# A decoder kernel: narrow attentions with queries and keys projected dimension-major and placed by way of DRAM

## The reference, cut to what matters

```
q = rope(x @ Wq)    k = rope(src @ Wk)    v = src @ Wv        # src: x, or the context
probs = softmax(q k^T / 4)                                    # causal in the self-attention
x = layernorm(x + (probs v) @ Wo)                             # cross-attention adds a bias
```

## Time and profile before

| | us |
|---|---|
| median of three runs (3670.48 to 3684.72) | 3678.97 |
| time of the profiled execution | 3678.92 |
| its span, first to last instruction | 3677.3 |
| PE busy / DVE / ACT / POOL | 3309.4 / 2046.3 / 1330.3 / 569.4 |

### The profile page before, as it was taken

One profiled execution on the slowest core, in us unless ns is written; L12 is line 12 of the kernel. 1 busy time (PEld: TensorE's weight loads), 2 busy tenths in 40 slices (PEclk: granted clock), 3 DMA queues, 4 the chain that ended last, 5 costly groups with the idle time before them and its releaser, 6 DMA issues. The chain is left out here.

```text
span 3677.3 us, 54612 instructions
## 1 busy us (share of the span) xinstructions
PE 3309.4 (90%) x19817; PEld 2550.5 (69%) x19818; DVE 2046.3 (56%) x4960; ACT 1330.3 (36%) x2944; POOL 569.4 (15%) x621
## 2 busy tenths in 40 slices
PE   7999999999999999987957899889898867999995
PEld 6889888888888788873425565545555435787784
DVE  3555655566666666632155666666667545343445
ACT  0444434443444344421113343435445443122110
POOL 1333322222222222024140111210000000000000
PEclk7999989999999999968988999989999978999998
DMA  5211110111111010024440000000000011000001
GB/s 190 53 53 53 53 53 30 35 35 30 30 35 35 28 31 30 1 104 160 137 119 32 2 3 2 28 2 22 5 5 5 2 46 24 24 12 11 23 11 46
DMA packets 110616, 146.80 MB, mean 40 GB/s; under 512 B 23712, under 2 KB 72864, under 8 KB 109288
## 3 DMA queue, kind: packets, MB, share of 16 engines
q1 hardware_dynamic: 95904, 110.80, 9.5%
q0 software_dynamic: 14480, 32.91, 2.9%
HBM read 100.55 MB, written 42.08 MB: 39 GB/s over the span
## 5 line engine op out<-in xcount | busy, mean ns | idle before, releaser
L554 ACT ACTIVATE probs_w<-probs_w,low_w 128x256 f32<-128x256 f32 (+1 forms) x512 | 242.9, 475 | 590.3 <-DVE low_w L599 590.3
L1861 DVE TENSOR_REDUCE mx_n<-bank 128x6 f32<-128x768 f32 (+1 forms) x256 | 279.8, 1093 | 148.8 <-PE bank L1638 78.5
L1769 ACT ACTIVATE probsT_n<-bank 128x768 f32<-128x768 f32 (+1 forms) x256 | 235.8, 921 | 273.1 <-PE bank L1650 272.7
L572 DVE TENSOR_TENSOR probsT_lo_w<-bank,probsT_hi_w 128x384 fp32r<-128x384 f32 (+1 forms) x256 | 159.7, 624 | 124.7 <-ACT probsT_hi_w L537 124.0
L518 PE MATMUL bank<-wo_hi_w,oT_hi_w 128*128 128x512 f32 x512 | 211.9, 414 | 2.1 <-issue 2.1
L1632 PE MATMUL bank<-kT_n,qT_n 48*128 48x256 f32 (+1 forms) x1024 | 123.5, 321 | 94.3 <-DVE mx_n L1861 91.5
L518 PE MATMUL bank<-wo_hi_w,oT_lo_w 128*128 128x512 f32 x512 | 204.8, 400 | 0.0
L518 PE MATMUL bank<-wo_lo_w,oT_hi_w 128*128 128x512 f32 x512 | 204.5, 400 | 0.0
L582 DVE TENSOR_SCALAR probs_w<-probs_w,inv_w 128x256 f32<-128x256 f32 (+1 forms) x512 | 189.1, 411 | 20.7 <-issue 0.9
L450 PE MATMUL bank<-xT_lo_w,wq_hi_w 128*128 128x512 f32 x512 | 162.1, 398 | 0.0
L2299 DVE SCALAR_TENSOR_TENSOR h<-bank,scale_now,silu 128x512 f32<-128x512 f32 x64 | 48.0, 750 | 201.6 <-PE bank L2192 201.6
(11 more groups left out here) (359 smaller groups left out, 8178.2 us busy)
## 6 DMA issues: line engine op xcount, KB each, us to landing
expert_rows<-ctxT_hi_w SPq DMA_DIRECT2D x20, 512.0 KB, 4.5
work_m<-expert_rows SPq DMA_DIRECT2D x40, 256.0 KB, 2.6
expert_products<-work_m POOLq DMA_DIRECT2D x40, 256.0 KB, 2.6
staging_w<-in_L_attn_Wq SPq DMA_DIRECT2D x32, 256.0 KB, 2.9
expert_table<-ctxT_hi_w SPq DMA_DIRECT2D x16, 512.0 KB, 5.6
staging_w<-in_L_attn_Wo SPq DMA_DIRECT2D x32, 256.0 KB, 2.6
staging_w<-in_L_xattn_Wq SPq DMA_DIRECT2D x32, 256.0 KB, 2.7
staging_w<-in_L_xattn_Wo SPq DMA_DIRECT2D x32, 256.0 KB, 2.6
```

What stands on the lines that cost most here:

```text
L554: last = act.activation(pr, pr, ACT.Exp, bias=low[:, n % ROUNDS_OF_PROBS, tile:tile + 1], scale=-1.0, accum_out=den[:, n % ROUNDS_OF_PROBS ...
L572: return dve.tensor_tensor(dst, src, hi.bitcast(FP32), ALU.subtract)
L1769: act.activation(probsT[:, turn_ % SLOT_PAIRS, :, 0:cols], scoreT[:, :, 0:cols], ACT.Exp, scale=SCALE)\
L1861: dve.tensor_reduce(to.rearrange("p t h -> p h t"), seen, AX.X, ALU.max).then_inc(s["scores_read"], 1)
```

## The change

Queries and keys are projected with their dimensions on the partitions and the tokens along the free axis (`turned`: the weights are loaded as the stationary operand, 256 tokens stream). ACT copies them to `raw`. The rotary partner of each row is fetched by DMA to `swapped` (`swap`: odd partitions to even and back; the self-attention's weights are reordered once by ACT so that partners are neighbours, `by_pair`). The tables of cosines and sines are spread by GpSimd and turned by PE to the same layout (`table`; once for all self items, once for each cross item). The turning and the split into high and low parts are done by DVE for the queries (`split_queries`, at steps 13 to 15) and by GpSimd for the keys (`split_keys`, steps 9 to 13), each on [128, chunks, 256]. `store` writes both parts to DRAM (`bounce`), `place` reads them back as the three copies of 16 rows in each half: six DMAs for keys, six for queries. All these transfers are issued on GpSimd's queue, between its maskings. `parts`, `rot`, `turn`, the transposes `kT`/`qT` and `rotate` go; the first scores of pair 0 wait for all placements of their item. v0 and v1 move to steps 1 and 3, xT to 4 and 5, keys to 6 and 7, queries to 9 and 11. SyncE's queue keeps the loads of the self weights and the negated maxima.

```diff
-            e = "dve" if name in ("k0", "k1", "q0", "q1", "h0", "h1", "h2", "h3", "out0", "out1") else "act"
+            e = "dve" if name in ("h0", "h1", "h2", "h3", "out0", "out1") else "act"
...
         if at == 0:
             put(a, f, ["h0", "h2"])
-            put(a, g, ["kT11"])
-            put(b, g, wide(g, "kT12", "kT13"))
-            put(b, g, ["q0"])
         elif at == 1:
             put(a, f, ["h1", "h3"])
+            put(b, g, ["v0"])
...
         elif at == 3:
-            put(a, g, ["q1"])
+            put(a, g, ["v1"])
         elif at == 4:
+            put(a, e, ["xT0"])
             put(b, f, ["out0"])
         elif at == 5:
-            put(a, g, ["qT00"])
-            put(b, g, ["qT01"])
+            put(a, e, ["xT1"])
+            put(b, e, wide(e, "ctxT", "table"))
         elif at == 6:
+            put(a, e, ["k0"])
             put(b, f, ["out1"])
         elif at == 7:
-            put(a, g, ["qT10"])
-            put(b, g, ["qT11", "qT02"])
+            put(b, e, wide(e, "k1"))
         elif at == 8:
             put(a, now, ["negC"])
-            put(b, g, ["qT03", "qT12"])
         elif at == 9:
-            put(a, g, ["v0"])
-            put(b, g, ["qT13"])
...
+            put(a, e, ["q0"])
         elif at == 11:
...
+            put(a, e, ["q1"])
         elif at == 14:
             put(a, g, ["negA"])
-            put(b, e, ["kT00"])
-        elif at == 15:
-            put(a, e, ["kT01"])
...
+            def split_keys(n, part):
...
+                c = dims_chunks(n)
+                a, b, high = raw["k"][:, 0:c, :], swapped["k"][:, 0:c, :], hi["k"][:, 0:c, :]
+                cos, sin = (tables[:, i, :].unsqueeze(1).to_broadcast([P, c, SEQ]) for i in range(2))
+                if part == 0:
+                    pool.wait_ge(s["prep_act"], uses.nth["table", n if cross(n) else 0])
+                    pool.wait_ge(s["k_swapped"], 32 * (n + 1))
+                    pool.tensor_tensor(a, a, cos, ALU.mult)
+                elif part == 1:
+                    pool.tensor_tensor(b, b, sin, ALU.mult)
+                elif part == 2:
+                    pool.tensor_tensor(a, a, b, ALU.add)
+                elif part == 3:
+                    pool.tensor_copy(high, a)
+                else:
+                    pool.tensor_tensor(a.bitcast(FP32R), a, high.bitcast(FP32), ALU.subtract).then_inc(s["k_split"], 1)
+                pool.drain()
...
+            def swap(name, n):
...
+                pool.wait_ge(s["prep_act"], uses.nth["q1" if name == "q" else k_uses(n)[-1], n])
+                chunks = DC if name == "q" else dims_chunks(n)
+                for i in range(2):
+                    pool.dma_start(swapped[name][i:P:2, 0:chunks, :], raw[name][1 - i:P:2, 0:chunks, :])\
+                      .then_inc(s[f"{name}_swapped"], 16)
...
+            def store(name, n):
...
+                pool.wait_ge(s[f"{name}_split"], n + 1)
+                if n >= 1:
+                    pool.wait_ge(s[f"{name}_placed"], 96 * n)
+                chunks = DC if name == "q" else dims_chunks(n)
+                for i, src in enumerate((hi[name].bitcast(FP32), raw[name])):
+                    pool.dma_start(bounce[name][i, 0:chunks, :, :].rearrange("c p t -> p c t"), src[:, 0:chunks, :])\
+                      .then_inc(s[f"{name}_stored"], 16)
...
+            def place(name, n, copies):
...
+                pool.wait_ge(s[f"{name}_stored"], 32 * (n + 1))
+                if n >= 2:
+                    pool.wait_ge(s["scoresT_ready"], 2 * PAIRS * (n - 1))
+                to = (qT if name == "q" else kT)[:, n % 2, :, :].bitcast(FP32)
+                for j, part in enumerate((0, 1, 0) if name == "q" else (0, 0, 1)):
+                    if j not in copies:
+                        continue
+                    for r in range(2):
+                        rows = slice(64 * r + HW * j, 64 * r + HW * j + HW)
+                        if name == "q" or cross(n):
+                            src = bounce[name][part].rearrange("c p t -> (c p) t").rearrange("(b r d) t -> r d b t", r=2, d=HW)[r]
+                            pool.dma_start(to[rows, :, :], src).then_inc(s[f"{name}_placed"], 16)
+                        else:
+                            src = bounce[name][part, 0].rearrange("(g d) t -> d g t", d=HW)
+                            pool.dma_start(to[rows, 0:8, :], src).then_inc(s[f"{name}_placed"], 16)
...
+            pool.memset(kT[:, :, :, :].bitcast(FP32), 1.0)
+            swap("k", 0)
+            swap("q", 0)
+            for part in range(5):
+                split_keys(0, part)
+            store("k", 0)
+            store("q", 0)
+            for n in range(-1, ITEMS):
+                for at in range(PAIRS):
+                    if 0 <= n < BATCH:
+                        hide(n, at)
+                    g, e = n + 1, n + 2
+                    if g < ITEMS:
+                        if at == 0 and n >= 0:
+                            store("q", g)
+                        if at in (1, 2):
+                            place("k", g, (0,) if at == 1 else (1, 2))
+                        if at in (3, 4):
+                            place("q", g, (0,) if at == 3 else (1, 2))
+                    if e < ITEMS:
+                        if at == 8:
+                            swap("k", e)
+                        if at == 12:
+                            swap("q", e)
+                        if at == 14:
+                            store("k", e)
...
+                    if e < ITEMS and 9 <= at < 14:
+                        split_keys(e, at - 9)
...
+            def turned(b, n, w, src, chunk, chunks):
...
+                for cc in range(chunks):
+                    last = pe.matmul(b, w[:, cc, chunk * P:(chunk + 1) * P], src[:, cc, :], start=(cc == 0), stop=(cc == chunks - 1))
+                return last
...
-                if pair % 4 == 0:
-                    read(f"qT0{pair // 4}", n)
-                    read(f"qT1{pair // 4}", n)
+                if pair == 0:
+                    pe.wait_ge(s["k_placed"], 96 * (n + 1))
+                    pe.wait_ge(s["q_placed"], 96 * (n + 1))
...
+            act.wait_ge(s["wk_loaded"], 16)
+            copy(by_pair(wk_all[:, 0:DC * P], "f"), by_pair(unturned[:, DC * DIM:DC * DIM + DC * P], "a")).then_inc(s["self_turned"], 1)
+            act.wait_ge(s["wq_loaded"], 16)
+            copy(by_pair(flat(wq[:, :, :]), "f"), by_pair(unturned[:, 0:DC * DIM], "a")).then_inc(s["self_turned"], 1)
...
+            def split_queries(n, part):
...
+                a, b, high = raw["q"][:, :, :], swapped["q"][:, :, :], hi["q"][:, :, :]
+                cos, sin = (tables[:, i, :].unsqueeze(1).to_broadcast([P, DC, SEQ]) for i in range(2))
+                if part == 0:
+                    dve.wait_ge(s["prep_act"], uses.nth["table", n if cross(n) else 0])
+                    dve.wait_ge(s["q_swapped"], 32 * (n + 1))
+                    dve.tensor_tensor(a, a, cos, ALU.mult)
+                    dve.tensor_tensor(b, b, sin, ALU.mult)
+                elif part == 1:
+                    dve.tensor_tensor(a, a, b, ALU.add)
+                    dve.drain()
+                    dve.tensor_copy(high, a)
                 else:
...
+                    dve.tensor_tensor(a.bitcast(FP32R), a, high.bitcast(FP32), ALU.subtract).then_inc(s["q_split"], 1)
                 dve.drain()
...
+                    if n + 2 < ITEMS and at in (13, 14, 15):
+                        split_queries(n + 2, at - 13)
```

More of the change, by code:

```diff
@@ L1524, in _ @@
                 .then_inc(s["ctx_loaded"], 16)
[L1526 to L1529, removed]
+            nothing = pool.to_reg(0.0)
             def hide(n, pair):
@@ L1537, in hide, with spread_tables @@
                     .then_inc(s["hidden"], 1)
[L1539 to L1544, removed]
+            def spread_tables(n):
+                if n >= 1:
+                    pool.wait_ge(s["k_stored"], 32 * n)
+                for i in range(2):
+                    for t in range(TILES):
+                        to = spread[:, P * (TILES * i + t):P * (TILES * i + t + 1)].rearrange("p (h w) -> p h w", h=8)
+                        if cross(n):
+                            last = pool.tensor_copy(to, (rotary.cos, rotary.sin)[i][:, batch_of(n) * TILES + t, :]
+                                                    .unsqueeze(1).to_broadcast([P, 8, HW]))
+                        else:
+                            one = chip.const[:, (C_COS, C_SIN)[i] + HW * t:(C_COS, C_SIN)[i] + HW * (t + 1)]
+                            for a in range(2):
+                                last = pool.tensor_copy(to[:, :, a::2], one[:, 8 * a:8 * a + 8].unsqueeze(1).to_broadcast([P, 8, 8]))
+                last.then_inc(s["table_spread"], 1)
@@ L1591, in prepare @@
                     last = four(b, lambda i: ctx_sb[:, i % 2, i // 2 * P:(i // 2 + 1) * P])
+                elif name == "table":
+                    pe.wait_ge(s["table_spread"], max(n - BATCH + 2, 1))
```

(19 more changed lines are left out.)

149 lines of the change are left out of this document (64 added, 85 removed).

## The result

The changed kernel takes 3745.25 us (median of four runs, 3742.91 to 3756.55) where the kernel before takes 3677.97 beside it: a ratio of 1.0189, 95% interval 1.0171 to 1.0207. That is 1.9% slower, 49 us above the forecast and just outside its range. The profiled execution has a span of 3741.5.

A forecast was written before the change was run, and what follows sets the result against it. PE bounds the kernel at nine tenths; after the change the placement loop would. 3679 + 33 (start) - 13 (cross items) - 3 (self items) = 3696 us, +0.5%; range 3580 to 3740, the forecast case's own 3665 to 3725.

The forecast's parts named there:

- item 3 of the loop: VectorE's query split and two maxima, 8.5 us in a cross item, plus 1.0 for GpSimd's key split running beside them.
- The rival of bulk transfers that delay one another: Stores queued with key stores and swaps take 2.7 us more in each of fifteen loops: 3737 us, chance 0.18.
- 58.1 for PE's own work: Cross iteration if only removed work counted: 67.0 less 9.5 for transposes, plus 0.6 for the table.
- `split_queries` would stall PE about as `rotate` did: Maxima of steps 13 to 15 wait behind the split; one stall set against the other, at nothing.
- The placement loop: From projecting keys and queries to next iteration's first scores; bounds the iteration, with pieces at 2.6 us each; chance 0.57.
- the loop of 65.4: Cross item's sum, projection through store and twelve pieces (31.2 us), above PE's own 58.1; gains 1.6 on 67.0.
- the point from which the loop decides: The stream's case was to decide from 2.4 us a piece downwards; forecast range 2.4 to 2.75 us a piece.
- the stream's rival: Placement pieces run as a stream at 1.45 us each, loops fall under PE's own work: 3580 us, chance 0.25.
- Self items: Loop of 57.4 us against 57.9 now, its twelve pieces taking 23.4; seven such iterations gain 3 us.
- masking holds the values for microseconds: Named sign of failure: masking queued behind GpSimd's DMA issues delays PE's values; forecast allowed half a us, left in rounding.
- The start: First scores move from 1956.6 to 1989.6, 33 us later, once; queries' store ends at 1966.2, then pieces take 23.4.
- the parts named for slower: Shares of the chance of slower: 0.27 from the forecast case, 0.16 from delayed bulk; stated total 0.44.

The follow-up runs named there:

- run 9: Changed kernel with only a cross item's key split moved from GpSimd to VectorE, pieces keeping their rows: 3700.2 us, 1.0065 to the kernel before.
- run 4: Changed kernel with GpSimd's five key operations in cross items on 8 of 256 tokens only: 3686.8 us, 1.0028 to the kernel before.
- run 2: Changed kernel with at most two placement pieces in flight in cross items and tables spread ahead of them: 3738.2 us, 1.0178 to the kernel before.
- run 5: Changed kernel with the three copies' rows interleaved, so a 16-partition piece reaches over 46: 3672.9 us, 0.9975 to the kernel before.
- run 7: Changed kernel with interleaved rows and a cross item's key split on VectorE: 3637.1 us, 0.9883 to the kernel before.
- run 3: Changed kernel with paced placements and the normalisation's last two parts moved later: 3720.8 us, 1.0131 to the kernel before.
- run 1: Changed kernel with the normalisation's last two parts moved from steps 9 and 10 to 11 and 12: 3720.8 us, 1.0135 to the kernel before.
- run 8: Kernel before, with five operations on a spare buffer added on GpSimd in each cross iteration: 3698.5 us, 1.0037 to the kernel before.

## Why the prediction was wrong

**The step that failed is item 3 of the loop, GpSimd's operations beside VectorE's.** It was priced at 1.0 us, "between nothing and one whole 2.6", and only where the queries' split stands. The runs show 7.8 us an iteration (74.6 to 66.8 with the keys on VectorE, run 9, which pays for them with some 6 us more of VectorE's time) to 9.8 (run 4). Each tensor operation of GpSimd's split can hold one of VectorE to its end; those held most were the tiny ones of the normalisation of the item before, which the sum didn't look at; and what followed was worse than the hold: 5.60 us of idle PE and 2.7 us of a slow projection. The Trainium skill, "SBUF — State Buffer", "Who interferes with whom", which the forecast cited, has the whole-instruction exclusion right; it applies to an operation of two elements as to one of 1,024.

**A wait was missing.** That the negated maxima pass through the same DMA engines as the pieces stood in no term. The rival of bulk transfers that delay one another named the mechanism but priced it on stores alone, at 2.7 us a loop; it was 5 us at negB and 2 more at the lower clock. Runs 2 and 5 remove it in two ways (a short queue, faster pieces), and run 5's iteration is 8.2 us shorter; run 4 shows that it doesn't hang on the key split. Why DMAs of a few KB on another queue take 14 us rather than one piece's 2.2 or the whole queue's 26, no run tells.

With both waits gone an iteration takes 59.3 us (run 7), so the forecast's 58.1 for PE's own work was near. That `split_queries` would stall PE about as `rotate` did was right too: PE waits for maxima 5.8 us an iteration in run 9 (41.8 us from 2440 to 2920) and 6.7 before (46.3 from 2440 to 2900).

**The placement loop was sized too long and, in cross items, does not bind.** In cross items pieces land 2.1 to 2.35 us apart, not 2.6. For twelve pieces that is some 5 us, and the loop of 65.4 becomes some 61. Run 9 lets it be estimated from its profile: iterations of 66.8 with first maxima 4.3 to 6.0 us after the last landing, where a bound loop has 1.1 (run 3), so some 63; the other terms were then some 2 us short. With the two holes an iteration takes 74.6, and first scores don't wait from the second cross item on. The forecast called 2.4 us the point from which the loop decides; the pieces were on the other side of it, and the stream's rival failed too, because the gain was taken by waits that neither case had.

**Self items** gain some 3.5 us an iteration in place of 0.5 (54.5 in the middle of the stage, against 57.9). The same piece price, 0.4 on six query pieces and half of that on six key pieces, takes 57.4 to 53.8. But with faster pieces (run 5) the iteration stays at 54.5, so PE's own work and its other waits are level with the loop there. One of those is a sign that the forecast itself had named as failure: masking holds the values for microseconds, 13.9 us in all, where it had half a us. The sum looked at POOL's issues ahead of a masking; the row above shows VectorE's split holding a masking, for about 1 us of PE's 1.75, and no run tests what that costs.

**The start** was right in its total, +33 forecast and +37 measured, with first scores at 1990.4 for 1989.6, but partly by luck: the queries' store had landed at 1971.8 and not 1966.2, and the pieces behind it took 18.6 us and not 23.4. One sum of the chances is off by a hundredth: the parts named for slower, 0.27 and 0.16, give 0.43 and not 0.44.

Shown by runs: the exclusion (1, 4, 7, 8, 9), the wait for negB (2, 5), the price of a piece by its partitions (5), the loop when it is stretched (2, 3). Read from the profile alone, with no run that changes it by itself: that the lower clock behind a hole is what lengthens the next pair, and that VectorE's split holds the maskings.

## What to carry to other kernels

When work is moved to GpSimd, list every operation of VectorE in those steps, the smallest too, and price each overlap at GpSimd's whole operation, then follow which engine the held one keeps waiting. When bulk transfers are added, ask which small transfers are wanted while they are queued, on whatever queue. And before a layout with few partitions a transfer is given up, see whether the order of rows is free: one line here turned 1.9% slower into 0.25% faster.

## What the runs showed of the hardware

Queued DMAs of 256 KB to 16 neighbouring partitions each moved at about 119 GB/s (changed kernel), to 16 partitions three apart at 140 to 220 (run 5). The Trainium skill, "SBUF — State Buffer", "Door 1: The DMA port swizzle", gives 104 GB/s for partitions 0 to 15 (four ports) and 189 for eight; the runs agree in kind, with the first some 14% quicker than its figure. An operation of VectorE with one tensor input (L130, two elements) is held by GpSimd as well, for up to 2.35 us (run 1), while maxima read from PSUM beside the same GpSimd operations keep 1.23. It goes the other way too: a masking of 0.64 us on GpSimd took 1.61 beside VectorE's split. A tensor operation of the key split takes 2.35 us on GpSimd and 1.23 on VectorE (run 7).
